# A graph attention stage on one core: running totals as a broadcast product and a sum, the order of one step, and three one-hot tiles on VectorE

## The chip, the cores and the metric

The kernel runs on one core of a Trainium2 chip as one launch. The metric is the device time of the whole program in microseconds. It is a network of four layers, each with a graph part and a mixture-of-experts part; the change touches the edge stage of layer 1's graph part.

## The reference

The graph has 3125 nodes and 50,000 edges, sorted by destination, and 3125 self loops, which layer 1 treats apart. Layer 1's graph part is an attention over the edges of each node, with 4 heads of 64 channels:

```
e      = x_l[src] + x_r[dst] + ea @ W_e            # per edge, 256 wide
e      = where(e > 0, e, 0.2 * e)                  # the bend
logits = einsum('ehc,hc->eh', e, att)              # 4 numbers per edge
m      = segment_max(logits, dst)
a      = exp(logits - m[dst])
out    = segment_sum(x_l[src] * a, dst) / segment_sum(a, dst)
```

Layer 3's graph part is the same with one head of 256 channels. It runs through the same function of the kernel.

## The kernel before, in words

`gat_edges` writes the edge stage for both layers. Edges are laid out in tiles of 128, a pair of tiles belongs to one block of 128 nodes, and a batch is four tiles, that is two pairs (k = 0 and 1). There are 110 batches. A batch needs its gathered rows of x_l (four indirect DMAs of GpSimd, L1122), a one-hot matrix per tile that says which of the block's nodes each edge belongs to (`onehot`), its turned form (`nodehot`), the logits, the running maximum per node and head (`top`), the powers, the weighted rows, and a running total per node (`total`, 4 heads of 64 channels and one column of the sum of powers, 260 wide).

The maximum runs: when it rises from one pair to the next, the total so far has to be shrunk. `shrink` holds that factor, 4 numbers per node (128x4). `add(k)` (L3411 on) takes the total of the other parity, shrinks it and adds what TensorE summed for this pair in `ps_s`. It is written as one instruction per head, so eight of 65 columns for a batch (L3422), each with a column of `shrink` as its scalar. ScalarE's `flush` then copies the total to the block's place in `net.work`.

Each engine runs its own list of stages in a loop over batches; `skewed` (L1173) writes it. A stage has a lag: at step t it works on batch t - lag. The order within the list is the order on the engine. Waits are semaphores. There is no planner; the order is written by hand. For layer 1 (four heads, so two units of two heads for each pair) it is, with the lags:

- VectorE: `hot` (1, two one-hot tiles, L1164), maxima of pair 0 (4, two instructions, L3388), `raise_first` (4, L3396), join of pair 0 (3, `vector_early`, L3637), maxima of pair 1 (4), `raise_second` (4, three 128x4 instructions, L3403, L3405, L3408), join of pair 1 and the bends of both pairs (3, `vector_middle`, L3637, L3642), totals of both pairs (5, L3422), logit sums of both pairs (3, `vector_late`, L3664).
- GpSimd: index cast (L1154) and the other two one-hot tiles (L1156), four gathers (L1122), and for the batch of two steps ago the product with `att`, one instruction of 128x512 per pair (L3659). The product of pair k waits for the bend of pair k, and the logit sum of pair k waits for the product.
- TensorE: rows of logits of pair 1 (3, L3464 and L3467), sums of weighted rows (4, L3478), `spread` (3, minus the logits plus the maximum for every edge, L3484 and L3486), `tensor` (1, edge sums for the joins, L3627 and L3628, which waits for `nodehot` of its batch), rows of logits of pair 0 (2), `turn` (0, turns the one-hot tiles, L3449).
- ScalarE: `shrinks` (3, L3513), `weigh` (3, L3517 and L3519, then 16 products L3528 and two copies L3531), `turn` (0, L3508 and L3509: `outside` and `nodehot`), `flush` (4, L3544 and L3545).
- SyncE: one load of edge records and one of edge attributes per batch.

The rows of logits alternate between two halves of `ps_row`, and each waits until the maxima before it have read the half. One sum `ps_s` and one set of edge sums `ps_x` exist for each k.

Of the kernel before, what the change touches and what calls it, by code (L numbers as in the profile page):

```python
# [12 lines left out]
ALU = mybir.AluOpType  # L13
# [3 lines left out]
P = 128  # L17
# [11 lines left out]
BATCH = 4  # L29
TWO = BATCH // 2  # L30
# [156 lines left out]
def tiled(ap, width):  # L187
    return ap.rearrange("p (t d) -> p t d", d=width)
# [892 lines left out]
class Gather:  # L1081

    def __init__(self, s, net, placed, table, width, lo):
        self.net, self.placed, self.table, self.width, self.lo, self.n = net, placed, table, width, lo, placed.width - lo
# [61 lines left out]
    def hot_tiles(self, eng, q, i, b, tick):  # L1150
        eng.wait_ge(self.rec_loaded[b], i * 16 + 16)
        eng.wait_ge(self.hot_free, q + 1)
        eng.sem_inc(tick, 1)
        eng.tensor_copy(self.idx[b][:, :], self.column(b, self.placed.far)).then_inc(self.idx_ready, 1)  # L1154
        for k in range(BATCH // 2):
            ins = eng.tensor_scalar(at(self.onehot[b], k, P), self.net.columns[:, :], self.column(b, self.placed.near, k),  # L1156
                                    None, ALU.is_equal)
        ins.then_inc(self.hot_ready, 1)

    def hot_half(self, eng, q, i, b):  # L1160
        wide = [P, BATCH // 2, P]
        eng.wait_ge(self.rec_loaded[b], i * 16 + 16)
        eng.wait_ge(self.hot_free, q + 1)
        eng.tensor_tensor(tiled(self.onehot[b][:, :], P)[:, BATCH // 2:BATCH, :],  # L1164
                          self.net.columns[:, :].unsqueeze(1).to_broadcast(wide),
                          self.column(b, self.placed.near)[:, BATCH // 2:BATCH].unsqueeze(2).to_broadcast(wide), ALU.is_equal)\
            .then_inc(self.half_ready, 1)

    def wait_rows(self, eng, i, b):
# [2124 lines left out]
def gat_edges(net, name, heads, each, table, lo, logits_of, tops=None):  # L3294
# [7 lines left out]
    W = heads * (each + 1)  # L3302
    UNITS = -(-heads // 2)
    FLUSH = 1 if tops is None else 2
    placed = net.by_dst
    with ExitStack() as ctx:
        s = net.scope(name, ctx)
# [10 lines left out]
        power = [s.sb(f"power{b}", [P, KH]) for b in range(RING)]  # L3318
        weighted = s.sb("weighted", [P, BATCH * W])
        total = [s.sb(f"total{k}", [P, W]) for k in range(TWO)]  # L3320
        ps_hot = s.ps("ps_hot", [P, BATCH * P])
        ps_x = s.ps("ps_x", [P, TWO, 512])
        ps_row = s.ps("ps_row", [P, 2, 512])
# [11 lines left out]
        shrink_ready = s.sem("shrink_ready")  # L3335
        spread_top = s.sem("spread_top")
        eased = s.sem("eased")
        shrunk = s.sem("shrunk")
        powered = s.sem("powered")
        weighted_ready = s.sem("weighted_ready")  # L3340
        summed = s.sem("summed")
# [21 lines left out]
        def _(dve):  # L3363
# [47 lines left out]
            def add(k):  # L3411

                def step(q, i, b):
                    n = q * TWO + k
                    if k == 0:
                        dve.wait_ge(shrunk, q + 1)
                    dve.wait_ge(summed, n + TWO + 1)
                    dve.wait_ge(flushed, (n + 1) * FLUSH)
                    dve.wait_ge(total_ready, n + TWO)
                    for h in range(heads):  # L3420
                        own = slice(h * (each + 1), (h + 1) * (each + 1))
                        ins = dve.scalar_tensor_tensor(total[k][:, own], total[1 - k][:, own], shrink[b][:, k * heads + h:k * heads + h + 1],  # L3422
                                                       ps_s[:, k, own], ALU.mult, ALU.add)
                    ins.then_inc(total_ready, 1)
                return 5, step

            units = [tops_of(k, h0) for k in range(TWO) for h0 in range(0, heads, 2)]
            early, middle, late, find, hot = ((lag, lambda q, i, b, part=part: part(dve, q, i, b)) for lag, part in
                                              zip((3, 3, 3, 0, 1), logits.vector_steps()))
            ends = (add(0), add(1), late) if UNITS > 1 else (late, hot, add(0), add(1))  # L3430
            if UNITS > 1:
                skewed(dve, hot, *units[:UNITS], (4, raise_first), early, *units[UNITS:], (4, raise_second), middle, *ends)
            else:
                skewed(dve, find, *units, (4, raise_first), early, (4, raise_second), middle, *ends)

        @block.tensor
        def _(pe):
# [43 lines left out]
            def spread(q, i, b):  # L3481
# [3 lines left out]
                for m in range(BATCH):  # L3485
# [3 lines left out]
                ins.then_inc(spread_top, 1)  # L3489


            skewed(pe, *([(3, turn_logits(1))] if UNITS > 1 else []), (4, add), (1, lambda q, i, b: logits.blocks(pe, q)), (3, spread),
                   (1, lambda q, i, b: logits.tensor(pe, q, i, b)), (2, turn_logits(0)),
                   *([(2, turn_logits(1))] if UNITS == 1 else []), (0, turn))

        @block.scalar
        def _(act):
# [14 lines left out]
                act.wait_ge(shrink_ready, q * TWO + TWO)  # L3512
                act.activation(shrink[b][:, :], shrink[b][:, :], ACT.Exp).then_inc(shrunk, 1)  # L3513

            def weigh(q, i, b):
                act.wait_ge(spread_top, q + 1)
                act.activation(power[b][:, :], ps_fall[:, :], ACT.Relu).then_inc(eased, 1)  # L3517
                act.wait_ge(eased, q + 2)
                act.activation(power[b][:, :], power[b][:, :], ACT.Exp, scale=-1.0).then_inc(powered, 1)  # L3519
                g.wait_rows(act, i, b)  # L3520
                act.wait_ge(powered, q + 1)
                for k in range(TWO):
                    act.wait_ge(summed, q * TWO + k + 1)
                    for m in (2 * k, 2 * k + 1):
                        out = by_head(at(weighted, m, W), each + 1)
                        for h in range(heads):
                            lo = m * g.width + h * each
                            act.activation(out[:, h, 0:each], g.rows[b][:, lo:lo + each], ACT.Copy,  # L3528
                                           scale=power[b][:, m * heads + h:m * heads + h + 1])
                    ones = by_head(at(weighted, k, 2 * W), each + 1)[:, :, each]  # L3530
                    act.activation(ones, at(power[b], k, 2 * heads), ACT.Copy).then_inc(weighted_ready, 1)  # L3531
                act.wait_ge(weighted_ready, q * TWO + TWO)
                act.sem_inc(g.rows_free, 1)

# [12 lines left out]
            skewed(act, (3, shrinks), (3, weigh), (0, turn), (4, flush))  # L3547


class L1Logits:  # L3550
# [254 lines left out]
class L1Finish:  # L3805
# [31 lines left out]
    def by_head(self, ap):  # L3837
        return ap.rearrange("p (n c) -> p n c", c=self.C)
# [655 lines left out]
```

## Time and profile before

| | |
|---|---|
| median of 3 runs | 6182.91 us (6182.76 to 6188.17) |
| the profiled execution | 6176.19 us |
| its span | 6174.6 us |
| PE, DVE, POOL, ACT busy over the span | 81%, 66%, 50%, 45% |
| layer 1's edge stage | from about 2190 to 3275 us of the span |

The busy shares of the span are averages over very different stages. The edge stage is 1085 of the 6175 us, and the DMA share there is low. In the rows, PE is TensorE's matmuls, PEld its weight loads, DVE is VectorE, ACT ScalarE, POOL GpSimd. A row that covers several instructions gives the time from the start of the first to the end of the last.

### The profile page before, as it was taken

How to read it: one execution, taken by the hardware profiler on the slowest of the kernel's cores; microseconds unless marked ns; L12 is line 12 of the kernel's file. 1: busy time of each engine (PE TensorE's matmuls, PEld its weight loads, DVE VectorE, ACT ScalarE, POOL GpSimd, SP SyncE). 2: the span in 40 equal slices, each digit the busy share in tenths (PEclk: the TensorE clock that was granted, in tenths of full speed). 3: DMA queues.
4: the chain of work that ended last, by engine and by line, in shares of the span. 5: the costliest groups of instructions: out<-in, count | busy, mean ns of one | idle time of the engine just before them, and what ended most of it. 6: DMA issues, size and time to landing. Idle time of an engine off the chain costs nothing. (4 is left out here: it accounts for less than half of the span.)

```text
span 6174.6 us, 119601 instructions
## 1 busy us (share of the span) xinstructions
PE 4978.6 (81%) x26396; PEld 3786.4 (61%) x26475; DVE 4081.7 (66%) x12578; ACT 2801.1 (45%) x8000; POOL 3087.3 (50%) x3487
## 2 busy tenths in 40 slices
PE   5720999998477779999993899969999997888695
PEld 4610677776354557777773677745657775777585
DVE  7771566665587779999996888754333336777612
ACT  0010777775115347777773111124533333787423
POOL 4787777775674068888880222213210002777221
PEclk9975999998696789999995999989989998999797
DMA  7521444445487222222231566544320002666453
GB/s 246 182 67 45 122 125 126 125 125 110 135 257 193 66 66 69 69 71 70 70 66 51 191 202 213 177 140 133 118 64 10 12 9 80 161 161 161 88 172 118
DMA packets 787155, 719.97 MB, mean 117 GB/s; under 512 B 349416, under 2 KB 693005, under 8 KB 786414
## 3 DMA queue, kind: packets, MB, share of 16 engines
q1 hardware_dynamic: 596376, 372.06, 21.2%
q0 software_dynamic: 120064, 280.26, 17.2%
q10 hardware_dynamic: 70486, 65.22, 3.0%
q8 instruction: 67, 1.10, 0.1%
q14 instruction: 162, 1.33, 0.1%
HBM read 520.74 MB, written 201.60 MB: 117 GB/s over the span
## 5 line engine op out<-in xcount | busy, mean ns | idle before, releaser
L1122 POOL DMA_INDIRECT l3e_rows<-table,l3e_idx x440 | 432.6, 983 | 733.8 <-DVE l3e_idx L1144 615.3
L1122 POOL DMA_INDIRECT l0e_rows<-table,l0e_idx x440 | 426.7, 970 | 154.3 <-issue 128.9
L1122 POOL DMA_INDIRECT l1e_rows<-table,l1e_idx x440 | 427.7, 972 | 121.4 <-issue 121.4
L890 POOL DMA_INDIRECT records_by_src<-l0n_rec_src,l0n_pos_at_src x390 | 398.0, 1020 | 115.4 <-issue 108.8
L3528 ACT ACTIVATE l1e_weighted<-l1e_rows,l1e_power 128x64 f32<-128x64 f32 x1760 | 442.6, 334 | 18.5 <-ACT l1e_power L3519 18.1
L1433 PE MATMUL l0e_ps_w<-l0e_wf,l0e_hidT 128*128 128x256 f32 x1760 | 435.3, 380 | 0.0
L3464 PE MATMUL l1e_ps_row<-net_ident,l1e_logit 128*128 128x128 f32 x1760 | 276.7, 280 | 82.4 <-DVE l1e_logit L3664 81.5
L1433 PEld LDWEIGHTS l0e_ps_w<-l0e_wf,l0e_hidT 128*128 128x128 f32 x1760 | 300.4, 191 | 63.0
L2168 ACT ACTIVATE l2fe_hT<-l2fe_ps_h,l2fe_own,l2fe_own 128x320 f32<-128x320 f32 x320 | 197.7, 618 | 310.7 <-PE l2fe_ps_h L2118 310.5
L3659 POOL TENSOR_TENSOR l1e_e<-l1e_e,l1x_att 128x512 f32<-128x512 f32 x220 | 313.8, 1446 | 29.2 <-DVE l1e_e L3642 21.5
L2827 ACT ACTIVATE l1fg_hT<-l1fg_ps_h,l1fg_b_cols 128x256 f32<-128x256 f32 x256 | 107.5, 471 | 458.0 <-PE l1fg_ps_h L2770 457.9
L1367 DVE SCALAR_TENSOR_TENSOR l0e_hidT<-l0e_ps_h,l0e_bf_low,l0e_raised 128x512 f32<-128x512 f32 x220 | 155.1, 746 | 227.6 <-ACT l0e_raised L1479 226.8
L2221 DVE SCALAR_TENSOR_TENSOR net_x<-l2fe_ps_y,l2fe_mix,net_x 128x256 f32 x200 | 96.7, 483 | 309.5 <-PE l2fe_ps_y L2130 309.5
L3388 DVE TENSOR_REDUCE l1e_tile_top<-l1e_ps_row 128x2 f32<-128x512 f32 x440 | 288.3, 685 | 16.1 <-PE l1e_ps_row L3467 3.5
L4057 PE MATMUL l2d_ps<-l2d_wide,net_work 128*128 128x512 f32 (+2 forms) x800 | 290.0, 518 | 8.6 <-DVE l2d_wide L4108 5.9
L3464 PEld LDWEIGHTS l1e_ps_row<-net_ident,l1e_logit 128*128 128x128 f32 x1760 | 191.6, 137 | 163.2 <-issue 110.7
L3478 PE MATMUL l3e_ps_s<-l3e_weighted,l3e_onehot 128*128 128x257 f32 x880 | 236.5, 414 | 53.1 <-ACT l3e_weighted L3531 52.6
L2951 POOL DMA_INDIRECT outputs<-l1fg_y,l1fg_target x64 | 66.3, 1035 | 404.0 <-DVE l1fg_y L2879 388.3
L3627 PE MATMUL l1e_ps_x<-l1x_xr,l1e_nodehot 128*128 x880 | 255.4, 392 | 2.8 <-ACT l1e_nodehot L3509 2.8
L2770 PE MATMUL l1fg_ps_h<-l1fg_xT,l1fg_w_in 128*128 128x256 f32 x1024 | 254.0, 381 | 0.8 <-issue 0.8
L3975 POOL DMA_DIRECT2D l2d_counts<-counts x192 | 107.1, 558 | 280.0 <-ACT l2d_wide L4167 139.9
L2784 PE MATMUL l1fg_ps_y<-l1fg_w_out,l1fg_hT 128*128 128x256 f32 x1024 | 241.5, 379 | 0.0
(857 smaller groups left out, 14927.0 us busy)
## 6 DMA issues: line engine op xcount, KB each, us to landing
counts<-l1f_total ACTq DMA_DIRECT2D x272, 128.0 KB, 4.4
l1fg_w_in<-in_L_ffn_W SPq DMA_DIRECT2D x32, 1024.0 KB
l1fg_w_out<-in_L_ffn_W SPq DMA_DIRECT2D x32, 1024.0 KB
records_by_dst<-l0n_blank_dst SPq DMA_DIRECT2D x5, 6512.0 KB
l3e_rec<-records_by_dst SPq DMA_DIRECT2D x110, 296.0 KB, 3.6
l2d_counts<-counts SPq DMA_DIRECT2D x208, 128.0 KB, 2.4
l2d_counts<-counts POOLq DMA_DIRECT2D x192, 128.0 KB
l3fg_w_in<-in_L_ffn_w SPq DMA_DIRECT2D x16, 1024.0 KB
```

The lines of the kernel that those rows point to most:

```text
L890: pool.indirect_dma_start(self.to.records, bass.IndirectOffsetOnAxis(self.pos_at[b][:, j:j + 1], 0), at(self.rec[b], j, self.to.width), No ...
L1122: pool.indirect_dma_start(at(self.rows[b], k, self.width), None, self.table, bass.IndirectOffsetOnAxis(self.idx[b][:, k:k + 1], 0)).then_i ...
L1433: ins = pe.matmul(ps_w[:, k, m * D:(m + 1) * D], hidT[b][:, c * WIDE + (2 * k + m) * P:c * WIDE + (2 * k + m + 1) * P], at(wf2, c, D), sta ...
L2770: ins = pe.matmul(ps_h[:, n % HALVES, (m % 2) * SLICE:(m % 2 + 1) * SLICE], w_in[b][:, c * F + m * P:c * F + (m + 1) * P], at(xT[b], c, SL ...
L2784: ins = pe.matmul(ps_y[:, t, 0:D], hT[b][:, c * SLICE + t * P:c * SLICE + (t + 1) * P], at(w_out[b], c, D), start=c == 0, stop=c == FC - 1)
L3388: dve.tensor_reduce(tile_top[:, c:c + w], tiled(ps_row[:, side, 0:w * PAIR], PAIR), AX.X, ALU.max)\
L3464: pe.matmul(ps_row[:, side, lo:lo + P], logit[b][:, c:c + 1].to_broadcast([P, P]), net.ident[:, :], is_transpose=True, start=h == h0 and m ...
L3478: ins = pe.matmul(ps_s[:, k, 0:W], at(g.onehot[b], m, P), at(weighted, m, W), start=m == 2 * k, stop=m > 2 * k)
L3528: act.activation(out[:, h, 0:each], g.rows[b][:, lo:lo + each], ACT.Copy, scale=power[b][:, m * heads + h:m * heads + h + 1])
L3627: pe.matmul(out, at(self.nodehot[b], 2 * k + m, P), at(self.xr, self.block[k], D), start=True, stop=False)
L3659: pool.tensor_tensor(e, e, self.att[:, :].unsqueeze(1).to_broadcast([P, 2, D]), ALU.mult).then_inc(self.times_att, 1)
L4057: ins = pe.matmul(ps[0:k_in, n % 2, 0:width(g)], lhsT, wide[k % WIDE][:, 0:width(g)], start=t == 0, stop=False)
```

## The change

Four things change, all of them for layer 1's edge stage. First, `add(k)` for more than one head no longer works head by head: a new stage `fade(k)` multiplies the whole total (260 wide) by `shrink`, broadcast over the 65 columns of each head, into a new tile `faded`, and `add(k)` adds `ps_s` to that in one instruction. Second, VectorE's list has a new order: join 0, join 1 and both bends follow each other, the maxima of pair 1 and `raise_second` come behind them, and the fades, adds and logit sums alternate, with the one-hot part ahead of the last add. Third, GpSimd makes one one-hot tile of the four and VectorE three, in one instruction of 384 columns. Fourth, TensorE's list has the edge sums (`tensor`) ahead of `spread` and the sums of weighted rows behind reading the block numbers. ScalarE's `weigh` is split into two functions that follow each other directly, so its order of work is the same. For one head the lists come out in the order they had.

```diff
-        for k in range(BATCH // 2):
+        for k in range(self.BY_POOL):                       # BY_POOL = 1
             ins = eng.tensor_scalar(at(self.onehot[b], k, P), self.net.columns[:, :], self.column(b, self.placed.near, k),
                                     None, ALU.is_equal)
...
-        wide = [P, BATCH // 2, P]
+        wide = [P, BATCH - self.BY_POOL, P]
...
                     n = q * TWO + k
+                    if heads > 1:
+                        dve.wait_ge(faded_ready, n + 1)
+                        dve.wait_ge(summed, n + TWO + 1)
+                        dve.wait_ge(flushed, (n + 1) * FLUSH)
+                        dve.tensor_tensor(total[k][:, :], faded[k][:, :], ps_s[:, k, 0:W], ALU.add).then_inc(total_ready, 1)
+                        return
...
+            def fade(k):
+
+                def step(q, i, b):
+                    n = q * TWO + k
+                    if k == 0:
+                        dve.wait_ge(shrunk, q + 1)
+                    dve.wait_ge(total_ready, n + TWO)
+                    dve.sem_inc(dve_tick, 1)
+                    dve.tensor_tensor(by_head(faded[k][:, :], each + 1), by_head(total[1 - k][:, :], each + 1),
+                                      at(shrink[b], k, heads).unsqueeze(2).to_broadcast([P, heads, each + 1]), ALU.mult).then_inc(faded_ready, 1)
+                return 5, step
...
-                skewed(dve, hot, *units[:UNITS], (4, raise_first), early, *units[UNITS:], (4, raise_second), middle, *ends)
+                skewed(dve, *units[:UNITS], (4, raise_first), early, middle, *units[UNITS:], (4, raise_second), fade(0), add(0), late, fade(1), hot, add(1))
...
-            skewed(pe, *([(3, turn_logits(1))] if UNITS > 1 else []), (4, add), (1, lambda q, i, b: logits.blocks(pe, q)), (3, spread),
-                   (1, lambda q, i, b: logits.tensor(pe, q, i, b)), (2, turn_logits(0)),
-                   *([(2, turn_logits(1))] if UNITS == 1 else []), (0, turn))
+            blocks, products = (1, lambda q, i, b: logits.blocks(pe, q)), (1, lambda q, i, b: logits.tensor(pe, q, i, b))
+            if UNITS > 1:
+                skewed(pe, (3, turn_logits(1)), blocks, (4, add), products, (3, spread), (2, turn_logits(0)), (0, turn))
+            else:
+                skewed(pe, (4, add), blocks, (3, spread), products, (2, turn_logits(0)), (2, turn_logits(1)), (0, turn))
```

## Rows read from the trace of the kernel before

**Rows 1.** Busy time of each engine in a stretch: us, then each engine's (x instructions)

```profile
core 0: us, PE busy (x) PEld busy (x) DVE busy (x) ACT busy (x) POOL busy (x), PEclk, DMA share, GB/s
2600.00:2800.00 200.00, 181.30 (x1137) 141.61 (x1136) 187.52 (x485) 142.72 (x569) 173.51 (x190) 1.00 0.27 70
```

**Rows 2.** One line's instructions: duration ns min/median/max, first and last start us

```profile
L3396 DVE SCALAR_TENSOR_TENSOR l1e_top<-l1e_top,l1e_fresh,l1e_tile_top x110: 221/222/225, 2224.1 to 3261.6; 128x4 f32<-128x4 f32 x110
```

**Rows 3.** Timeline of VectorE, one step: start us, us, what, [idle before]

```profile
2611.92 0.41 DVE L1164 TENSOR_TENSOR l1e_onehot<-net_columns,l1e_rec 128x256 f32<-128x256 f32 x1
2612.46 1.34 DVE L3388 TENSOR_REDUCE l1e_tile_top<-l1e_ps_row 128x2 f32<-128x512 f32 x2
2613.95 0.22 DVE L3396 SCALAR_TENSOR_TENSOR l1e_top<-l1e_top,l1e_fresh,l1e_tile_top 128x4 f32<-128x4 f32 x1
2614.19 0.69 DVE L3637 TENSOR_TENSOR l1e_e<-l1e_ps_x,l1e_rows 128x512 f32<-128x512 f32 x1
2614.80 1.28 DVE L3388 TENSOR_REDUCE l1e_tile_top<-l1e_ps_row 128x2 f32<-128x512 f32 x2
2616.22 0.22 DVE L3403 SCALAR_TENSOR_TENSOR l1e_top<-l1e_top,l1e_fresh,l1e_tile_top 128x4 f32<-128x4 f32 x1
...
2616.63 0.68 DVE L3637 TENSOR_TENSOR l1e_e<-l1e_ps_x,l1e_rows 128x512 f32<-128x512 f32 x1
2617.23 1.28 DVE L3642 SCALAR_TENSOR_TENSOR l1e_e<-l1e_e 128x512 f32<-128x512 f32 x2
2618.43 1.82 DVE L3422 SCALAR_TENSOR_TENSOR l1e_total<-l1e_total,l1e_shrink,l1e_ps_s 128x65 f32<-128x65 f32 x8
2620.17 1.42 DVE L3664 TENSOR_REDUCE l1e_logit<-l1e_e 128x8 f32<-128x512 f32 x2
2621.51 0.41 DVE L1164 TENSOR_TENSOR l1e_onehot<-net_columns,l1e_rec 128x256 f32<-128x256 f32 x1
```

**Rows 4.** The maxima as a group (busy, mean ns, idle before); timeline ahead of one

```profile
L3388 DVE TENSOR_REDUCE l1e_tile_top<-l1e_ps_row 128x2 f32<-128x512 f32 x421 | 275.7, 685 | 13.4 <-PE l1e_ps_row L3467 0.8
...
2610.60 1.40 DVE L3664 TENSOR_REDUCE l1e_logit<-l1e_e 128x8 f32<-128x512 f32 x2
...
2611.41 0.65 PE L3464 MATMUL l1e_ps_row<-net_ident,l1e_logit 128*128 128x128 f32 x4 [0.69 <-DVE l1e_logit L3664]
```

**Rows 5.** Timeline of GpSimd, one step

```profile
2610.01 1.27 POOL L3659 TENSOR_TENSOR l1e_e<-l1e_e,l1x_att 128x512 f32<-128x512 f32 x1
2611.23 0.18 POOL L1154 CAST l1e_idx<-l1e_rec 128x4 int32<-128x4 f32 x1
2611.40 1.40 POOL L1156 TENSOR_SCALAR l1e_onehot<-net_columns,l1e_rec 128x128 f32<-128x128 f32 x2
...
2618.00 1.65 POOL L3659 TENSOR_TENSOR l1e_e<-l1e_e,l1x_att 128x512 f32<-128x512 f32 x1 [0.24 <-DVE l1e_e L3642]
```

**Rows 6.** Timeline of TensorE and ScalarE, one step; waits of layer 3

```profile
2607.17 0.40 PE L3484 MATMUL l1e_ps_fall<-l1e_logit,l1e_minus 128*128 128x16 f32 x2 [0.17 <-DVE l1e_shrink L3408]
...
2608.31 0.68 PE L3627 MATMUL l1e_ps_x<-l1x_xr,l1e_nodehot 128*128 x2
...
2608.49 0.18 ACT L3517 ACTIVATE l1e_power<-l1e_ps_fall 128x16 f32<-128x16 f32 x1 [1.13 <-PE l1e_ps_fall L3486]
...
2610.45 0.27 PE L3628 MATMUL l1e_ps_x<-l1e_we_parts,l1e_attrT 128*128 128x256 bf16 x1
...
2613.41 0.60 ACT L3508 ACTIVATE l1e_outside<-l1e_ps_hot 128x512 bf16<-128x512 f32 x1 [0.18 <-PE l1e_ps_hot L3449]
2613.90 0.59 ACT L3509 ACTIVATE l1e_nodehot<-l1e_ps_hot 128x512 f32<-128x512 f32 x1
...
  ACT l3e_weighted L3531: 19.6, 98
```

**Rows 7.** A cast of VectorE beside a long GpSimd instruction in layer 2

```profile
4214.05 13.72 POOL L4125 TENSOR_TENSOR net_x<-net_x,l2d_last_bias 128x6400 f32<-128x6400 f32 x1
4214.53 13.54 DVE L4108 CAST l2d_wide<-l2d_counts 128x512 f32<-128x512 uint16 x1 [1.29 <-DMA l2d_kept<-counts]
...
L4108 DVE CAST l2d_wide<-l2d_counts x200: 407/427/13539, 4131.0 to 4546.4; 128x512 f32<-128x512 uint16 x100
```

More of the change, by code:

```diff
@@ L1081 @@
 class Gather:
+    BY_POOL = 1
     def __init__(self, s, net, placed, table, width, lo):
@@ L1160, in hot_half @@
     def hot_half(self, eng, q, i, b):
-        wide = [P, BATCH // 2, P]
+        wide = [P, BATCH - self.BY_POOL, P]
         eng.wait_ge(self.rec_loaded[b], i * 16 + 16)
         eng.wait_ge(self.hot_free, q + 1)
-        eng.tensor_tensor(tiled(self.onehot[b][:, :], P)[:, BATCH // 2:BATCH, :],
+        eng.tensor_tensor(tiled(self.onehot[b][:, :], P)[:, self.BY_POOL:BATCH, :],
                           self.net.columns[:, :].unsqueeze(1).to_broadcast(wide),
-                          self.column(b, self.placed.near)[:, BATCH // 2:BATCH].unsqueeze(2).to_broadcast(wide), ALU.is_equal)\
+                          self.column(b, self.placed.near)[:, self.BY_POOL:BATCH].unsqueeze(2).to_broadcast(wide), ALU.is_equal)\
             .then_inc(self.half_ready, 1)
@@ L3320, in gat_edges @@
         total = [s.sb(f"total{k}", [P, W]) for k in range(TWO)]
+        faded = [s.sb(f"faded{k}", [P, W]) for k in range(TWO)]
         ps_hot = s.ps("ps_hot", [P, BATCH * P])
@@ L3337, in gat_edges @@
         eased = s.sem("eased")
+        faded_ready = s.sem("faded_ready")
         shrunk = s.sem("shrunk")
@@ L3429, in _ @@
                                               zip((3, 3, 3, 0, 1), logits.vector_steps()))
-            ends = (add(0), add(1), late) if UNITS > 1 else (late, hot, add(0), add(1))
             if UNITS > 1:
-                skewed(dve, hot, *units[:UNITS], (4, raise_first), early, *units[UNITS:], (4, raise_second), middle, *ends)
+                skewed(dve, *units[:UNITS], (4, raise_first), early, middle, *units[UNITS:], (4, raise_second), fade(0), add(0), late, fade(1), hot, add(1))
             else:
-                skewed(dve, find, *units, (4, raise_first), early, (4, raise_second), middle, *ends)
+                skewed(dve, find, *units, (4, raise_first), early, (4, raise_second), middle, late, hot, add(0), add(1))
         @block.tensor
@@ L3513, in shrinks, with weigh_first @@
                 act.activation(shrink[b][:, :], shrink[b][:, :], ACT.Exp).then_inc(shrunk, 1)
-            def weigh(q, i, b):
+            def weigh_first(q, i, b):
                 act.wait_ge(spread_top, q + 1)
@@ L3521, in weigh, with weigh_pair @@
                 act.wait_ge(powered, q + 1)
-                for k in range(TWO):
+                weigh_pair(q, b, 0)
+            def weigh_pair(q, b, k):
                     act.wait_ge(summed, q * TWO + k + 1)
@@ L3531, in weigh, with weigh_second @@
                     act.activation(ones, at(power[b], k, 2 * heads), ACT.Copy).then_inc(weighted_ready, 1)
+            def weigh_second(q, i, b):
+                weigh_pair(q, b, 1)
                 act.wait_ge(weighted_ready, q * TWO + TWO)
@@ L3545, in flush @@
                     act.activation(at(net.work, blk, W), total[k][:, :], ACT.Copy).then_inc(flushed, 1)
-            skewed(act, (3, shrinks), (3, weigh), (0, turn), (4, flush))
+            skewed(act, (3, shrinks), (3, weigh_first), (3, weigh_second), (0, turn), (4, flush))
 class L1Logits:
```

## The prediction

> **What bounds the kernel now.** I read the busy table by stretch first. Inside layer 1's edge stage VectorE is busy 94% of the time, TensorE 91% at full granted clock, GpSimd 87%, ScalarE 71%; DMA moves 27% of its share [rows 1]. So three engines could bound it, and only the order of one step tells which. A step handles one batch of four edge tiles; there are 110. The first raising of the maxima starts at 2224.1 us and the last at 3261.6 [rows 2], which makes 1037.5 / 109 = 9.52 us a step. The reader is to see in VectorE's timeline that its rows follow without holes: hot 0.54 (start to start), two tile maxima 1.49, raise 0.24, join 0.61, two maxima 1.42, three small ones 0.41, join 0.60, two bends 1.20, totals 1.74, two logit sums 1.34 [rows 3], altogether 9.59; this is one of the longer steps. The only idle time is some 0.13 us a step in front of the first maximum (13.4 us over 105 steps), where TensorE's rows come late [rows 4]. VectorE bounds, and GpSimd is right behind it: from the index cast at 2611.23 to the next multiply at 2618.00 is 6.77 us, 0.24 of it waiting, and the two multiplies add about 2.83 (1.65 and 1.27, starts to starts) [rows 5].
>
> **The change part by part, on VectorE.** Starts are spaced by duration less about 0.08 (0.68 against 0.60 for 512 columns [rows 3]), since instructions overlap.
> Totals: eight 65-wide instructions go, 1.74 us. In come two products and two sums 260 wide. No row has one. The nearest are 0.415 us for 256 columns with the same kind of broadcast (the hot rows) and 0.68 for 512 [rows 3]; bounds 0.28 (65 wide) and 0.68, and I take 0.42, so 0.34 of spacing each. The first sum stands directly behind its product and must wait for it: the restart costs about 0.13 instead of an overlap of 0.08, as in front of the raises (maxima end 2616.08, raise 2616.22 [rows 3]). Four times 0.34 plus 0.21 is 1.57; saved: 0.17.
> Hot: three tiles instead of two. 384 columns lie between 0.415 and 0.68; 0.55, so 0.13 more.
> Order: the bends directly behind the joins cost nothing by themselves. Logit sums and one-hot part now stand with a product and a sum between TensorE's request and the next maxima. TensorE starts 0.13 after the first logit sum (2610.60 + 0.68; its wait of 0.69 ends at 2611.41) and the first maximum 1.05 after that [rows 3, 4]. With logit sum 0 ended at +7.43 the rows are there at +8.61, and the next step starts only at +9.10: the 0.13 of idle goes, and 0.06 of the late second maximum with it.
> Laid out from the first maximum: raise +1.44 (0.18 to the join, between the 0.14 of the small ones and the 0.24 above), joins +1.62 and +2.22, bends +2.82 and +3.42, second maxima +4.02 and +4.62, raises +5.45 to +5.86, product 0 +5.86, sum 0 +6.41, logit sums +6.75 and +7.35, product 1 +7.95, hot +8.29, sum 1 +8.76, end +9.10, with the loop's overhead 9.13. If nothing else changed, that would be 0.39 a step less.
> GpSimd gives up one one-hot tile, 0.60 to 0.70 us (1.40 for two [rows 5]); it then needs 6.77 - 0.24 - 0.65 + 2.83 = 8.71 and bounds nothing. Its gathers start 0.6 earlier behind the cast; nobody waits for rows now and nobody will. SyncE's two loads a step stay as they are. Layer 3's edge stage keeps its order of work on all engines; it counts at nothing.
>
> **What GpSimd's multiply does to what now stands beside it.** This decides. The multiply reads two tensors from SBUF. Its times come in pairs: 1.65 for the first of a batch, 1.27 for the second [rows 5]. The first starts at 2618.00, while the second bend (two SBUF inputs) runs from 2617.83 to 2618.51 [rows 3, 5], and is 0.38 longer; the second lies beside totals, which read SBUF once and PSUM once, and takes 0.38 less. So a VectorE instruction with two SBUF inputs that came first holds GpSimd up. The reverse order stands once in this trace: the cast that takes 0.43 us in the median started 0.48 us into GpSimd's 13.72 us tensor_tensor and took 13.54: it ended 0.30 after it, as if started 0.13 before its end [rows 7].
> In the kernel before, no VectorE instruction with two SBUF inputs starts during a multiply. After the change four do: bend 0 ends at +3.50, multiply 0 starts at +3.59 (0.09 later, as now), is held by bend 1, ends at about +5.23; multiply 1 runs +5.20 to +6.47. The three small ones due at +5.45 read `top` and `tile_top` from SBUF. If they are held, the first gets going at 6.47 - 0.13 = +6.34: 0.89 late. Everything behind follows. Product 0 (two SBUF inputs) then comes at about +6.75, beside GpSimd's cast and one-hot tile (+6.42 to +7.2): 0 to 0.45 more, I take 0.10. Step: 9.13 + 0.89 + 0.10 = 10.12 us.
> The bounds of this cost: nothing held, 0; all held until the one-hot tile is done, 0.89 + 0.45 = 1.34, a step of 10.47.
> The Trainium skill states the case that the rows lack: SBUF — State Buffer, section "Who interferes with whom", says that a VectorE instruction with two SBUF inputs contends with a GpSimd instruction that reads SBUF, and that whoever issues second is blocked for the other's whole instruction. By it the raises and product 0 are held, without it only 2-port casts would be. The trace agrees in what it shows: bend before multiply costs GpSimd 0.38, beside sums with one SBUF input it has its shorter time.
>
> **A second limit, without VectorE.** TensorE's order is new: the edge sums ahead of the spread (tensor before spread). Now the spread's result goes to ScalarE, which eases, raises and weighs, then copies the next nodehot; the edge sums of the following TensorE step wait for that copy, and the spread stands behind them. That closes a loop of one step: spread 2607.17 to ScalarE's start 2608.49, to the end of nodehot 2613.90 + 0.59 = 2614.49 [rows 6], so 7.32; 0.05 to TensorE; edge sums 2608.31 to the start of the last matmul at 2610.45 and 0.11 more, 2.25 [rows 6]. Sum 9.62. The 0.18 idle before 2613.41 doesn't go away: it is marked as waiting for TensorE, but layer 3 has the same gap, 19.6 us in 98 steps, with nothing but ScalarE's own last instruction in front of it [rows 6]. Before the change the spread came first and the loop had two steps of time. So even where VectorE would be ready at 9.13, a step is no shorter than 9.62, 0.10 above today's. It lies hidden under 10.12.
>
> **Sum.** VectorE bound at 10.12: 0.60 us more in each of 109 steps, 65 us. The profiled execution took 6176.2 us (span 6174.6), 6.7 below the median of 6182.9: 6241 against it, 6248 against the median.
>
> **The rivals.**
> A, the holding doesn't reach these instructions (it needs a 2-port form as the cast has, or tiny instructions slip through). For it: only the cast's row shows VectorE blocked. Against: the bends hold the multiply, and they are of the same form as the raises. Then the ScalarE-TensorE loop decides: 9.62, +10 us, 6193.
> B, the other side, faster: nothing is held and the loop comes out shorter than I read it, as its weight loads and the ACT gaps overlap more behind edge sums than behind an idle TensorE. Then VectorE's 9.13 is the step: -0.39 x 109 = -43 us, 6140. For it: VectorE is the bound today and has less to do. Against: the loop would have to lose 0.1 us to break even and 0.2 to be told from no change, and each of its terms is a row. It decides below 9.41.
> C, held in part: the raises wait, but multiply 1 lets go sooner, or GpSimd is shifted; step 9.7 to 9.9, +20 to +41 us, 6203 to 6224.
> D, the products don't cost what I take: at 0.68 instead of 0.42 each they add up to 1.0 us a step to VectorE, beyond 10.4 even unheld. Rows of two widths speak against it.
>
> **Chances.** Forecast 0.68, its own range 6228 to 6290 (steps of 9.93 to 10.5). A 0.13, B 0.10, C 0.07, D 0.02. A measurement of this kernel tells changes above 0.2%, 12 us. A splits: 0.10 within, 0.03 slower; B: 0.08 faster, 0.02 within. Faster 0.08, same 0.12, slower 0.80. The range leaves out B, half of A and some tail: 6190 to 6288.
>
> **What would show it.** Right: the first second-raise (or the small one behind it) at about 1.1 us instead of 0.22, beginning inside multiply 1; raises 10.1 apart; the first multiply still 1.65; ScalarE idle grown by 0.6 a step; DVE's four 260-wide at 0.42. A: raises 0.22 long, steps of 9.6, VectorE idle ahead of the first maxima on `ps_row`, and TensorE's edge sums waiting for nodehot. B: steps of 9.1 to 9.4 and no such waits. The forecast is wrong if the small instructions keep their 0.22 us inside a multiply.

## The result and the profile after

The changed kernel takes 6238.6 us (6236.8 to 6240.3, 4 runs) against 6182.8 (6174.7 to 6188.2, 4 runs) for the kernel before, a ratio of 1.0091 (95% interval 1.0077 to 1.0105): 0.9% slower. The forecast was 6248 with the range 6190 to 6288. The medians lie 55.8 us apart. The profiled execution has a span of 6238.5 us, 63.9 more than before. One execution of experiment 1's kernel took 9348.8 us at a granted clock of 0.73 and is left out of its ratio, while the 6212.4 us given there is the median of all five.

The first view is the one of [rows 1], the busy time of each engine over the same 200 us inside the edge stage of layer 1.

```profile
core 0: us, PE busy (x) PEld busy (x) DVE busy (x) ACT busy (x) POOL busy (x), PEclk, DMA share, GB/s
2600.00:2800.00 200.00, 176.03 (x1075) 135.18 (x1074) 192.42 (x378) 134.18 (x537) 149.83 (x160) 0.99 0.25 65
```

VectorE is busier than before (192.4 against 187.5 us) although fewer steps pass. TensorE, ScalarE and GpSimd each do less. So VectorE still bounds, and something has made its step longer. The next view is that of [rows 2], two of VectorE's lines: the first raise, and the first of the three small instructions of pair 1 (before, 221 ns in the median and 225 at most).

```profile
L3397 DVE SCALAR_TENSOR_TENSOR l1e_top<-l1e_top,l1e_fresh,l1e_tile_top x110: 221/223/225, 2224.8 to 3320.3; 128x4 f32<-128x4 f32 x110
L3404 DVE SCALAR_TENSOR_TENSOR l1e_top<-l1e_top,l1e_fresh,l1e_tile_top x110: 221/1036/2669, 2228.7 to 3322.8; 128x4 f32<-128x4 f32 x110
```

From the first start to the last are now 1095.5 us, 10.05 a step against 9.52. These 0.53 us in 109 steps are 58 of the 64 us; the rest lies outside these steps and was not sought. The same form of instruction, 4 numbers per partition, takes 0.22 us in one place and 1.04 in the median in the other. The grouped view (busy us, mean ns, idle before) of the stage from 2250 to 3300 us shows where the other changed terms lie.

```profile
L3684 POOL TENSOR_TENSOR l1e_e<-l1e_e,l1x_att 128x512 f32<-128x512 f32 x208 | 280.6, 1371 | 7.6 <-DVE l1e_e L3667 5.1
L3389 DVE TENSOR_REDUCE l1e_tile_top<-l1e_ps_row 128x2 f32<-128x512 f32 x418 | 268.1, 683 | 1.2 <-PE l1e_ps_row L3485 1.1
L3404 DVE SCALAR_TENSOR_TENSOR l1e_top<-l1e_top,l1e_fresh,l1e_tile_top 128x4 f32<-128x4 f32 x104 | 128.9, 1240 | 14.7
L3442 DVE TENSOR_TENSOR l1e_faded<-l1e_total,l1e_shrink 128x260 f32<-128x260 f32 x210 | 89.7, 427 | 0.0
L3420 DVE TENSOR_TENSOR l1e_total<-l1e_faded,l1e_ps_s 128x260 f32<-128x260 f32 x210 | 88.4, 421 | 7.2 <-DVE l1e_faded L3442 4.3
L1163 DVE TENSOR_TENSOR l1e_onehot<-net_columns,l1e_rec 128x384 f32<-128x384 f32 x105 | 57.7, 550 | 0.0
L1153 POOL CAST l1e_idx<-l1e_rec 128x4 int32<-128x4 f32 x104 | 19.5, 187 | 126.5 <-PE l1e_ps_fall L3504 126.5
```

Products and sums cost 0.43 and 0.42 us, 384 columns 0.55, and the idle time ahead of the maxima has gone (1.2 us, before 13.4 [rows 4]). The raise lasts 1.24 us in the mean. The last row shows a wait that is new: GpSimd's cast waits 1.2 us a step for the spread. Before, GpSimd's order of one step showed no such wait [rows 5], and none stands in the list of GpSimd's waits for the whole stage.

One step in the timelines of VectorE, GpSimd and TensorE (start us, us, idle before), which answers to [rows 3, 5, 6]:

```profile
2610.68 1.43 DVE L3404 SCALAR_TENSOR_TENSOR l1e_top<-l1e_top,l1e_fresh,l1e_tile_top 128x4 f32<-128x4 f32 x1
2612.03 0.21 DVE L3406 SCALAR_TENSOR_TENSOR l1e_shrink<-l1e_top,l1e_fresh 128x4 f32<-128x4 f32 x1
2612.17 0.21 DVE L3409 SCALAR_TENSOR_TENSOR l1e_shrink<-l1e_top,l1e_fresh 128x4 f32<-128x4 f32 x1
2612.30 0.43 DVE L3442 TENSOR_TENSOR l1e_faded<-l1e_total,l1e_shrink 128x260 f32<-128x260 f32 x1
...
2603.33 0.19 POOL L1153 CAST l1e_idx<-l1e_rec 128x4 int32<-128x4 f32 x1 [1.38 <-PE l1e_ps_fall L3504]
...
2608.30 1.27 POOL L1121 DMA_INDIRECT l1e_rows<-table,l1e_idx  x1 [0.31 <-issue]
2609.58 2.50 POOL L3684 TENSOR_TENSOR l1e_e<-l1e_e,l1x_att 128x512 f32<-128x512 f32 x2
2613.22 0.19 POOL L1153 CAST l1e_idx<-l1e_rec 128x4 int32<-128x4 f32 x1 [1.13 <-PE l1e_ps_fall L3504]
...
2612.44 0.39 PE L3502 MATMUL l1e_ps_fall<-l1e_logit,l1e_minus 128*128 128x16 f32 x2
```

The raise starts inside the two multiplies, which end at 2609.58 + 2.50 = 2612.08, and itself ends at 2612.11. Of the 110 raises 65 start 0.25 us into the second multiply or close to it and take 1.0 to 1.1 us; 38 start, as here, 1.1 us into the first and take 1.4. A held instruction is no gap in the trace: it shows as a long duration. The two small ones behind it cost 0.21 each, so only the first of the queue pays. Product 0 at 2612.30 is free, for GpSimd is idle until 2613.22, waiting for the spread that the held raise has delayed.

### The profile page after: what moved, and what is told of

Its sections match the earlier page's. It is cut to its first block and busy times, and to the rows that moved or that the text cites. A ratio compares the mean times of both kernels' runs of the same rounds, so it can differ in the third digit from the quotient of the medians.

```text
span 6238.5 us, 119182 instructions
## 1 busy us (share of the span) xinstructions
PE 5013.2 (80%) x26396; PEld 3798.2 (61%) x26475; DVE 4165.3 (67%) x12138; ACT 2801.1 (45%) x8000; POOL 3016.5 (48%) x3377
## 5 line engine op out<-in xcount | busy, mean ns | idle before, releaser
L1121 POOL DMA_INDIRECT l1e_rows<-table,l1e_idx x440 | 449.3, 1021 | 131.4 <-issue 131.4
L3684 POOL TENSOR_TENSOR l1e_e<-l1e_e,l1x_att 128x512 f32<-128x512 f32 x220 | 296.7, 1371 | 21.5 <-DVE l1e_e L3667 19.0
L3496 PE MATMUL l1e_ps_s<-l1e_weighted,l1e_onehot 128*128 128x260 f32 x880 | 221.0, 394 | 81.9 <-issue 61.1
L3496 PEld LDWEIGHTS l1e_ps_s<-l1e_weighted,l1e_onehot 128*128 128x128 f32 x880 | 159.1, 191 | 140.7 <-issue 90.4
```

The costliest lines, as they stand in the source:

```text
L1121: pool.indirect_dma_start(at(self.rows[b], k, self.width), None, self.table, bass.IndirectOffsetOnAxis(self.idx[b][:, k:k + 1], 0)).then_i ...
L3496: ins = pe.matmul(ps_s[:, k, 0:W], at(g.onehot[b], m, P), at(weighted, m, W), start=m == 2 * k, stop=m > 2 * k)
L3684: pool.tensor_tensor(e, e, self.att[:, :].unsqueeze(1).to_broadcast([P, 2, D]), ALU.mult).then_inc(self.times_att, 1)
```

## The experiments

All ratios are against the kernel before, measured on the same chip, with the 95% interval; "a step" is the mean distance of the first raises over 109 steps. Each diff gives the main lines of an experiment.

**1. Is it the multiply's reading?** (changed kernel)

```diff
-            pool.tensor_tensor(e, e, att..., ALU.mult).then_inc(self.times_att, 1)
+            pool.sem_inc(self.pool_tick, 1)
+            pool.memset(self.scratch[k][:, :], 0.0).then_inc(self.times_att, 1)   # 1300 columns of its own
```

> The changed kernel, but GpSimd's product with att (two SBUF inputs) is replaced by a write of zeros to a tile of its own, 1300 columns, about as long (estimate 1.2 us); the product is left out. Holding theory: GpSimd reads no SBUF there, so the first small raise of the second pair (1.0 to 1.4 us, mean 1.24, in the changed kernel) is back at 0.22. The step then isn't VectorE's 9.13 but the loop ScalarE-TensorE, 9.62: about 6193 us. Rival 1, the raise is long for another reason (its semaphore, its place behind the maxima): it stays at 1.2, steps of 10.05, 6238 us. Rival 2, no loop decides and VectorE alone does: 9.13, 6140 us.

6212.4 us, 1.0045 (1.0029 to 1.0061), a step 9.76. Rows of the group view and of the waits (us in total, times, longest):

```profile
L3686 POOL MEMSET l1e_scratch<- 128x1300 f32 x212 | 245.9, 1199 | 13.7 <-DVE l1e_e L3668 13.6
L3404 DVE SCALAR_TENSOR_TENSOR l1e_top<-l1e_top,l1e_fresh,l1e_tile_top 128x4 f32<-128x4 f32 x107 | 23.8, 222 | 14.8
...
DVE l1e_tile_top L3389 <- PE l1e_ps_row L3485: 59.8, 99, 1.2
PE l1e_ps_x L3653 <- ACT l1e_nodehot L3529: 34.9, 100, 0.5
```

GpSimd is as long at work (1.20 us against 1.27), and the raise again starts inside it, mostly 0.5 us in. But GpSimd only writes, and the raise is back at 222 ns. So the holding comes with GpSimd's reading, not with its being busy. What is left is not VectorE's bound: it now waits for rows, and the edge sums wait for nodehot. The hidden loop decides, at 9.76 instead of the 9.62 worked out.

**2. The same with TensorE's order of before** (sums of weighted rows, blocks, spread, edge sums)

> As e1_write_only (the product left out), and TensorE in the order of before: spread ahead of the edge sums. Theory: raise 0.22. The loop ScalarE-TensorE of one step is open again, but another closes, since the raises now stand late in VectorE's step: raises done at +5.86, 0.06, spread 1.14, edge sums 2.25, rows 1.05 to the first maxima of the next step: 10.36 a step, about 6274 us. Rival: TensorE's order costs nothing either way, then as e1_write_only, and if e1's 9.62 came from the order alone, 9.13, 6140 us.

6465.0 us, 1.0457 (1.0440 to 1.0475). Steps of 10.37 to 10.49, as expected, stand beside steps of 13.7 to 13.8; the mean is 12.14. Four stretches of busy time, the next to last column the granted clock:

```profile
2616.00:2620.00 4.00, 1.95 (x13) 1.46 (x12) 3.83 (x10) 1.16 (x6) 2.38 (x3) 1.00 0.28 63
...
2652.00:2656.00 4.00, 3.89 (x16) 3.16 (x17) 3.16 (x8) 1.95 (x9) 2.64 (x5) 0.57 0.09 22
...
2664.00:2668.00 4.00, 2.07 (x11) 2.08 (x12) 3.64 (x10) 0.21 (x1) 2.78 (x5) 0.78 0.01 3
2668.00:2672.00 4.00, 4.00 (x11) 2.58 (x12) 1.27 (x4) 3.77 (x17) 3.08 (x4) 0.50 0.23 66
```

In both kinds of step TensorE has a stretch in which it is half idle (busy 1.95 and 2.07 of 4 us), waiting for the raise. In the steps of 10.4 the granted clock is 1.00 throughout. Stretches of four to six of them alternate over the whole stage with as many of 13.7 to 13.8, in which the clock is 0.75 in the mean and falls at times to the lower of its two levels (0.50 is 1.2 GHz): 3.3 us more. That price stood in no term of mine, and the 6274 us that I expected were missed by 191. So TensorE's new order is what lets the late raises be borne at all.

**3. Does one input of GpSimd hold too?**

```diff
-            pool.tensor_tensor(e, e, att..., ALU.mult).then_inc(self.times_att, 1)
+            pool.tensor_scalar(self.e[k][:, :], self.e[k][:, :], 1.5, None, ALU.mult).then_inc(self.times_att, 1)
```

> The changed kernel, but GpSimd's product with att is a product with a constant in place (one SBUF input, one SBUF output; the reference's product is left out). If any GpSimd instruction that reads SBUF holds a VectorE instruction with two SBUF inputs, the small raise stays near the end of GpSimd's second instruction: still 0.5 us or more, depending on how long the one-input instruction takes (estimate 0.9 to 1.3 us). If only two-input GpSimd instructions hold, the raise is 0.22 and the step is the loop's 9.62, 6193 us. If held, between 9.62 and 10.05: 6195 to 6238 us.

6224.9 us, 1.0066 (1.0050 to 1.0083), a step 9.83.

```profile
L3404 DVE SCALAR_TENSOR_TENSOR l1e_top<-l1e_top,l1e_fresh,l1e_tile_top 128x4 f32<-128x4 f32 x107 | 75.0, 701 | 14.8
L3409 DVE SCALAR_TENSOR_TENSOR l1e_shrink<-l1e_top,l1e_fresh 128x4 f32<-128x4 f32 x107 | 36.8, 344 | 0.0
```

One tensor read by GpSimd holds two-input instructions of VectorE too, but not as two do. Two steps of VectorE and GpSimd side by side:

```profile
2620.41 0.22 DVE L3404 SCALAR_TENSOR_TENSOR l1e_top<-l1e_top,l1e_fresh,l1e_tile_top 128x4 f32<-128x4 f32 x1
2619.92 3.16 POOL L3685 TENSOR_SCALAR l1e_e<-l1e_e 128x512 f32<-128x512 f32 x2
...
2630.41 1.02 DVE L3404 SCALAR_TENSOR_TENSOR l1e_top<-l1e_top,l1e_fresh,l1e_tile_top 128x4 f32<-128x4 f32 x1
2629.31 2.98 POOL L3685 TENSOR_SCALAR l1e_e<-l1e_e 128x512 f32<-128x512 f32 x2
```

A raise that starts 0.5 us into the first of GpSimd's two instructions (1.52 us each) takes its 0.22 us; one that starts 1.1 us into it takes 1.02 and ends 0.85 us before the second is done. Of 110 raises 60 are of this kind, and 33 that start inside an instruction are free. With two tensors read, every raise that starts inside the multiplies is held to their end. Before the change the two meet as well: GpSimd's one-hot tiles read SBUF, and VectorE's hot, two SBUF inputs, starts in the first of them (2611.92 in 2611.40 to 2612.80 [rows 3, 5]) and takes its 0.41 us; there it is GpSimd's second tile that takes longer (0.80 us against 0.61 for the first, medians of the stage). The Trainium skill, "SBUF — State Buffer", section "Who interferes with whom", sets GpSimd's instructions that read against those that only write. Experiment 1 agrees about the write. Of reading it says contention without a difference between one tensor and two, and with one these rows show a hold in part or none.

**4. TensorE's new order alone** (kernel before)

> The kernel before with one part of the change alone: TensorE has the edge sums ahead of the spread. Theory: this closes the loop spread, ScalarE's easing, powers, products, nodehot, edge sums, spread, in one step: 7.32 + 0.05 + 2.25 = 9.62 against 9.52 today: +11 us, 6194 us, the idle time of TensorE ahead of the edge sums ending with nodehot. Rival: the loop has slack that I don't see; 9.52, 6183 us.

6213.8 us, 1.0049 (1.0032 to 1.0066), a step 9.78: the loop by itself, with nothing else changed. Measured in one step: spread to ScalarE's start 1.21, to the end of nodehot 6.00, to the first edge sum 0.29, to the next spread 2.27, together 9.77. The prediction had 0.05 where 0.29 is. In this time TensorE's sequencer runs two instructions of its own that stand in front of the load of nodehot's first piece as weights: one at 2608.92 (L3623, a count on a semaphore), 0.04 after nodehot's end, and one with registers at 2609.07 (L3629); the load starts at 2609.16. In the kernel before, the same two pass at 2607.35 and 2607.49 while the spread is still at work, and the load follows the spread without a gap. That they make the 0.29 is read from this order and wasn't tested. The wait is in the trace:

```profile
PE l1e_ps_x L3629 <- ACT l1e_nodehot L3511: 35.9, 103, 0.4
```

**5. GpSimd keeps two one-hot tiles** (changed kernel, `BY_POOL = 2`)

> The changed kernel with two one-hot tiles on GpSimd and two on VectorE, as before. In the changed kernel GpSimd's cast waits for TensorE's spread, which waits for the held raise, which waits for GpSimd's second multiply: a loop of 9.89 us from cast to cast in a step whose raise is held 1.42. If this loop decides, 0.62 us more on GpSimd make the multiplies later by that and the hold longer: steps of about 10.5, 6183 + 0.98 x 109 = 6290 us, raise above 1.5 us on the mean. Rival: VectorE's own sum plus a fixed hold decides; it has 0.13 less to do: steps of 9.92, 6225 us.

6296.2 us, 1.0181 (1.0164 to 1.0198), a step 10.52, as the loop had it. GpSimd's multiplies come later; the raise now mostly starts 0.5 us into the first of them and ends with the second, 2.03 us in the median:

```profile
L3404 DVE SCALAR_TENSOR_TENSOR l1e_top<-l1e_top,l1e_fresh,l1e_tile_top 128x4 f32<-128x4 f32 x100 | 178.3, 1783 | 14.2
```

**6. Cast and first gather ahead of the wait for the spread** (changed kernel)

```diff
-        eng.wait_ge(self.hot_free, q + 1)
-        eng.sem_inc(tick, 1)
-        eng.tensor_copy(self.idx[b][:, :], self.column(b, self.placed.far)).then_inc(self.idx_ready, 1)
+        eng.sem_inc(tick, 1)
+        eng.tensor_copy(self.idx[b][:, :], self.column(b, self.placed.far)).then_inc(self.idx_ready, 1)
+        self.gather_batch(eng, q, b, range(1))
+        eng.wait_ge(self.hot_free, q + 1)
...
+        self.gather_batch(eng, q, b, range(1, BATCH))   # behind the one-hot tile
```

> The changed kernel, but GpSimd casts the indices and starts the first gather before it waits for the one-hot tile to be free (spread). Loop theory: GpSimd no longer waits behind the spread, its multiply 0 starts right behind bend 0 in each step (held by bend 1, 1.65 us), and the raise is held for the short time, 1.03, in each step: VectorE's sum 8.93 and 0.81, 9.74, and the loop ScalarE-TensorE allows 9.78: 9.78, 6183 + 0.26 x 109 = 6211 us. The steps of 12 us go too. Rival: GpSimd's wait for the spread is hidden: 10.05, 6239 us as the changed kernel.

6222.9 us, 1.0061 (1.0044 to 1.0078), a step 9.91. That lies between the theory (9.78) and the rival (10.05); the median step is 9.79, and longer ones, up to 11.9, still lift the mean. In 104 of 110 steps the first multiply again starts 0.1 us behind its bend, and the hold falls:

```profile
L3408 DVE SCALAR_TENSOR_TENSOR l1e_top<-l1e_top,l1e_fresh,l1e_tile_top 128x4 f32<-128x4 f32 x106 | 113.9, 1074 | 14.9
L1153 POOL CAST l1e_idx<-l1e_rec 128x4 int32<-128x4 f32 x104 | 19.3, 186 | 0.0
```

So the changed kernel has a loop of its own: cast, one-hot, gathers, multiplies, held raise, spread, cast, 2603.33 to 2613.22 in the step shown above. A raise held longer delays the multiplies that hold the next one. Cutting it gives 0.14 us a step, and GpSimd's wait for the spread is gone.

**7. Maxima and raises of pair 1 back ahead of join 1 and the bends** (changed kernel)

> The changed kernel, with the maxima and raises of pair 1 ahead of join 1 and the bends, as before; the rest of the new order stays, so product 0 follows bend 1 directly. Theory: the raises have 0.22 us again, but product 0 (two SBUF inputs) now meets multiply 0: either it is held (above 1 us instead of 0.42), or it goes first and multiply 0 takes 2.0 us. And the window beside the multiplies, 2.96 us from the end of bend 0, holds only about 2.0 us of VectorE's work, so VectorE waits for the second multiply: 8.93 + 0.96, with what is held 9.9 to 10.5 a step: 6225 to 6290 us. Rival: only tiny instructions are held; product 0 takes 0.42, multiply 0 1.65, and without the hold the step is the loop's 9.78: 6211 us.

6265.3 us, 1.0130 (1.0113 to 1.0147), a step 10.24. The raises take 222 ns, and the first product is held instead; the mean over both products is

```profile
L3442 DVE TENSOR_TENSOR l1e_faded<-l1e_total,l1e_shrink 128x260 f32<-128x260 f32 x205 | 195.6, 954 | 0.0
```

1.50 for product 0 and 0.42 for product 1 in the step read. Whichever two-input instruction stands there pays.

**8. The totals alone** (kernel before, product and sum in the place of the eight)

> The kernel before with one part of the change alone: totals as a product and a sum per pair, in the place of the old totals (product 0, sum 0, product 1, sum 1 behind the bends), so beside the multiplies. Theory: both products have two SBUF inputs and meet the multiplies: product 0 meets multiply 0, product 1 meets multiply 1 and waits for its end; the logit sums come 1.0 to 1.5 us later than before: steps of 10.5 to 11.0, 6290 to 6345 us, a product on the mean above 0.8 us. Rival: products aren't held, the totals are 0.17 us shorter, the step 9.4 to 9.52: 6170 to 6183 us.

6415.3 us, 1.0373 (1.0355 to 1.0390), a step 11.6, worse than either expectation. Both products are held (1.50 and 0.81 in the step read), and TensorE waits for the logit sums behind them. The granted clock is 0.94 from 2600 to 2800 us, 1.00 in the kernel before, so part of the time is the clock's; the run doesn't separate it.

```profile
L3442 DVE TENSOR_TENSOR l1e_faded<-l1e_total,l1e_shrink 128x260 f32<-128x260 f32 x180 | 204.0, 1134 | 13.2
L3482 PE MATMUL l1e_ps_row<-net_ident,l1e_logit 128*128 128x128 f32 x1440 | 256.9, 308 | 205.1 <-DVE l1e_logit L3689 205.1
```

The eight instructions that were replaced read one tensor from PSUM and one from SBUF and lay in the multiplies unharmed (1.82 us for the eight [rows 3]). That was their worth.

**9. One one-hot tile fewer on GpSimd, alone** (kernel before)

> The kernel before with one part of the change alone: one one-hot tile on GpSimd, three on VectorE. VectorE's hot part takes 0.13 more, but stands in front of the first maxima, where VectorE waits 0.13 for TensorE's rows; GpSimd has 0.65 less, and its multiply 0 still starts behind bend 0. Theory: 9.52 a step, 6178 to 6188 us. Rival: GpSimd bounds before the change (0.24 of waiting in one step only) and its 0.65 less shorten the step to 9.40: 6170 us; or VectorE's 0.13 count in full: 9.65, 6197 us.

6188.9 us against 6189.5, 1.0002 (0.9992 to 1.0011): nothing that can be told. VectorE's 0.13 more takes the place of most of the idle time ahead of the maxima (2.8 us in 107 steps, before 13.4 in 105). A step 9.57.

**10. An order in which nothing meets the multiplies.** VectorE: maxima 0, first raise, product 0, hot, joins, bends, maxima 1, sum 0, logit sums, raises of pair 1, product 1, sum 1. On TensorE the turning of the one-hot tiles stands between the two pairs' sums and the spread ahead of the edge sums; on ScalarE that turning and the flush go ahead of shrinking and weighing.

> A version after the theory: the changed kernel with an order in which no VectorE instruction with two SBUF inputs stands beside a multiply, and without the one-step loop of ScalarE and TensorE. VectorE: maxima 0, raise, product 0, hot, joins, bends, maxima 1, sum 0, logit sums, raises 1, product 1, sum 1. TensorE: rows 1, sums 0, turn of the batch before, sums 1, rows 0, spread, edge sums. ScalarE: turn of the batch before and flush ahead of the shrinks and weighing. Theory: raises 0.22, products 0.42; from the end of bend 0 to logit sum 1 VectorE has 2.63 us of work where the multiplies need 2.96, so 0.33 of waiting; step 8.95 to 9.3 us: -25 to -60 us, 6123 to 6158 us. Rival 1, the limit is elsewhere (TensorE at 8.6 of work a step now has the rows, spread and edge sums in a chain): 9.5 or more, 6183 us or above. Rival 2, holding explained only part: raises or products still above 0.5 us.

6344.9 us, 1.0243 (1.0229 to 1.0257): my forecast was wrong, the first rival right. Nothing is held (raises of pair 1 0.21 to 0.22, products 0.43), yet a step takes 10.9, at a granted clock of 0.89 from 2600 to 2800 us. The waits:

```profile
ACT l_top L3569 <- DVE l1e_total L3420: 323.5, 110, 5.1
POOL l1e_idx L1153 <- PE l1e_ps_fall L3504: 208.6, 96, 3.3
PE l1e_ps_row L3482 <- DVE l1e_logit L3692: 129.4, 89, 3.0
DVE l1e_logit L3692 <- POOL l1e_e L3687: 126.6, 178, 2.5
```

Late raises make a late spread, that a late cast, and so late multiplies for which VectorE then waits; or the flush does it. Two further kernels look into this.

**11. The same with experiment 6's edit, and logit sum 1 behind the raises of pair 1.**

```diff
-... *units[UNITS:], add(0), late, (4, raise_second), fade(1), add(1))
+... *units[UNITS:], add(0), late(0), (4, raise_second), late(1), fade(1), add(1))
```

> The order in which no VectorE instruction with two SBUF inputs lies in a multiply (steps of 10.9 us in the mean, GpSimd's cast waiting 2.2 us a step for the spread, the multiplies starting 1.3 us behind their bends), with two further edits: index cast and first gather go ahead of the wait for the spread, and the logit sum of pair 1 comes behind the raises of pair 1 instead of ahead of them. Theory (the late multiplies made that version slow, through the cast): the multiplies start within 0.2 us of the bends again, VectorE no longer waits for them (0.7 us a step goes), the raises come 0.67 us earlier and with them spread, ScalarE and nodehot: steps of 9.5 to 10.0 us, 6175 to 6235 us. Rival: TensorE's and ScalarE's own order makes it slow (flush waits for the totals of pair 1, 2.8 us a step, and ScalarE has all shrinking and weighing behind that): steps stay above 10.4, 6280 us or more, with the cast no longer waiting. A step below 9.4 and a time below 6170 would make it faster than the kernel before; I give that 1 in 6.

6176.5 us (6172.3 to 6184.1, 10 runs) against 6186.9 (13 runs), 0.9980 (0.9971 to 0.9990): 0.2% faster than the kernel before. The time is at the lower end of what was expected, the step of 9.41 in the mean (9.25 in the median) below it; the 6170 us and 9.4 to which I gave 1 in 6 were not reached.

```profile
L3408 DVE SCALAR_TENSOR_TENSOR l1e_top<-l1e_top,l1e_fresh,l1e_tile_top 128x4 f32<-128x4 f32 x107 | 59.3, 554 | 0.0
L1153 POOL CAST l1e_idx<-l1e_rec 128x4 int32<-128x4 f32 x103 | 19.0, 184 | 0.0
...
DVE l1e_logit L3696 <- POOL l1e_e L3691: 7.5, 4, 1.9
ACT l_top L3573 <- DVE l1e_total L3424: 240.4, 119, 4.2
```

The cast waits no more, and VectorE waits for the multiplies 4 times instead of 178. The flush still waits 2.0 us a time (2.9 in experiment 10) without harm, so it wasn't the cause. Which of the two edits did more isn't shown, and the granted clock is back at 1.00. The raise is now earlier than the end of multiply 1 by a little and held 0.33 us a step. Four steps of 11.4 to 11.6 us remain, 25 apart; in each a gather starts 2.7 us after the end of the one before it, where 0.3 is usual (see the last section).

**12. The same with TensorE's order of before, ScalarE's of the changed kernel.**

> The same VectorE and GpSimd order as in the run before, but with TensorE's order of the kernel before (sums of weighted rows first, spread ahead of the edge sums) and ScalarE's order of the changed kernel (flush last). Theory: without the edge sums ahead of the spread the loop spread, ScalarE, nodehot, edge sums, spread is two steps long again, and flush waits for nothing; what is left is the path raise, spread, edge sums, first join of the next step, which is closed by VectorE's list: from the raise 0.5 to the spread, 0.4 for it, 2.7 for edge sums and their weights, 0.1 to join 0, and from join 0 to the raise behind logit sum 0 about 5.3: 9.0 us, under VectorE's own 9.1. Steps of 9.2 to 9.9 us, 6150 to 6225 us. Rival: the raise that has moved behind logit sum 0 makes the spread so late that the edge sums hold up the joins and the rows of logits; each such wait lowers TensorE's granted clock and the steps go over 10.4, as with the old TensorE order before: 6280 us or more.

6686.0 us, 1.0802 (1.0784 to 1.0820), a step 14.1, the clock 0.84 in the mean from 2600 to 2800 us. The rival was right, and the lower clock is part of it:

```profile
DVE l1e_tile_top L3393 <- PE l1e_ps_row L3489: 342.2, 68, 6.4
PE l1e_ps_fall L3506 <- DVE l1e_shrink L3413: 245.4, 67, 3.7
```

With the spread ahead of the edge sums, a late raise holds up edge sums, joins, rows and maxima in turn. My 9.0 us for this path left out the rows of logits behind it and the clock; how much is due to each wasn't measured.

## Why the prediction was right

**The holding** was named with its place, victim and end, and it is what decides: taken away (experiment 1) the raise is at 222 ns, moved off the raise (7) or put on the totals alone (8) it falls on the product. I took 0.89 us a step from [rows 5, 7]; it is 1.24 - 0.22 = 1.02. The sum had the raise at one fixed place in the multiplies. It is held 0.8 where the first multiply started at the first bend's end, as the prediction laid it out, and 1.2 where GpSimd was late. The first multiply took its 1.65 in 48 of 110 steps; the prediction had it in all.

**VectorE's sum** without holding was put at 9.13; 10.05 less 1.02 leaves 9.03, a remainder and not a measurement of its own. The widths between known rows came out as taken (0.42 and 0.43 for 0.42, 0.55 for 0.55).

**Product 0's 0.10** did not come. The prediction had GpSimd begin its cast at once behind the multiplies; it waits for the spread. Nor would the one-hot tile have held the product: in experiment 3, 63 products start inside such a tile and all take 0.42. So what the prediction took to hold raises and product alike fits the raises behind the multiply, and not a two-input instruction beside the one-hot tile. The wait for the spread is the step that was missed: the raise holds the spread, the spread the cast, the cast the next multiplies. Experiment 6 prices it at 0.14 us a step. The errors are -0.10, +0.13 and -0.10, and 10.12 became 10.05; in time 58 us for 65. That they partly cancel is luck: the 0.13 is what the missed loop added and what four steps with a late gather added. The mechanism is not.

**The loop of 9.62**, hidden under the forecast, is really 9.76 to 9.78 (experiments 1 and 4): 0.24 more from nodehot's end to the first edge sum, 0.11 less from spread to nodehot's end, 0.02 more for the edge sums. Rival A, put at 6193, was experiment 1's 6212, and rival B could not come with this order of TensorE. Rival D's sum was wrong as it stands: 0.68 for each of four instructions is 1.0 us more, 9.13 + 1.04 = 10.17 unheld, not beyond 10.4; as 0.42 and 0.43 were measured, nothing hung on it.

**What each part does.** TensorE's order alone costs 30 us (4), the totals alone 229, part of it by the lower clock (8), the one-hot tile nothing (9). These don't add up: the new VectorE order moves the raises, not the products, into the multiplies, and TensorE's order makes that bearable (2).

## What to carry to other kernels

Before an instruction is moved or merged, write down what GpSimd runs at that time, how many tensors it reads from SBUF, and how many of the instruction's inputs lie there: here a PSUM operand was cover, and a tiny instruction queued behind GpSimd's two-tensor read lost as much as a large one (0.8 to 1.2 us against 1.07). A removed hold gives back only what the longest closed loop that is left allows (in experiment 1 spread, ScalarE, nodehot, edge sums), so follow each semaphore once round the step before counting a gain. Experiments 10 and 11 differ only in the start of another loop (raise, spread, cast, gathers, multiply) and one logit sum, and their steps by 1.5 us.

## What the runs showed of the hardware that was not expected

- A raise that comes in the last 0.2 us of the first multiply (the 1.43 above) waits for the whole second, and so does one that comes 0.5 us into the first (2.03 us in experiment 5). So a waiting VectorE instruction does not get its turn between two multiplies of two inputs that follow each other directly. Between two instructions of one input it does (experiment 3).
- Four raises of 110 took 2.66 to 2.67 us, to the end of both multiplies, although each started 0.15 us before the first multiply's recorded start. They lie 25 steps apart, and in each of the four steps a gather starts 1.5 us late on GpSimd, with nothing in the profile that it waited for (here the first). In every kernel of this document it is each hundredth gather. GpSimd's idle time ahead of it is 1.11 us in the kernel before, where it lengthens no step by more than 0.1, 1.83 in the changed kernel and 2.66 in experiment 11; 0.31 is usual. What held it stays open:

```profile
2474.93 0.94 POOL L1121 DMA_INDIRECT l1e_rows<-table,l1e_idx  x1 [1.83 <-issue]
...
2478.61 2.67 DVE L3404 SCALAR_TENSOR_TENSOR l1e_top<-l1e_top,l1e_fresh,l1e_tile_top 128x4 f32<-128x4 f32 x1
2478.76 2.49 POOL L3684 TENSOR_TENSOR l1e_e<-l1e_e,l1x_att 128x512 f32<-128x512 f32 x2
```

- From nodehot's end to the first matmul that needs it as weights, 0.29 us, where TensorE's sequencer had its two instructions still to run (experiment 4).
- In experiment 2 TensorE's granted clock went between 1.00 and 0.75 in the mean of a step, in a kernel in which TensorE waited part of each step, and the steps at 0.75 were 3.3 us longer.
